# Graph attention: the turns of a group's head on VectorE, and the head's five pieces behind batches 4 to 8

## The reference

```python
h = (x @ W_i).reshape(n, H, C)
es = jnp.einsum('nhc,hc->nh', h, a_src_i)
ed = jnp.einsum('nhc,hc->nh', h, a_dst_i)
e = es[src] + ed[dst]
e = jnp.where(e > 0, e, NEG_SLOPE * e)
m = jax.ops.segment_max(e, dst, num_segments=n)
p = jnp.exp(e - m[dst])
denom = jax.ops.segment_sum(p, dst, num_segments=n)
alpha = p / denom[dst]
msg = alpha[:, :, None] * h[src]
out = jax.ops.segment_sum(msg, dst, num_segments=n)
```

## Time and profile before

| what | before |
|---|---|
| median of 3 runs | 10096.06 us (10090.6 to 10096.87) |
| the profiled execution | 10127.15 us |
| its span in the profile | 10125.4 us |
| granted TensorE clock, mean | 0.63 |
| PE, DVE, ACT, POOL busy | 55%, 52%, 46%, 49% |
| DMA | 985 MB, mean 97 GB/s |

### The profile page before, as it was taken

One profiled execution on the slowest core, in us unless ns is written; L12 is line 12 of the kernel. 1 busy time (PEld: TensorE's weight loads), 2 busy tenths in 40 slices (PEclk: granted clock), 3 DMA queues, 4 the chain that ended last, 5 costly groups with the idle time before them and its releaser, 6 DMA issues.

```text
span 10125.4 us, 129123 instructions
## 1 busy us (share of the span) xinstructions
PE 5609.1 (55%) x33883; PEld 4488.5 (44%) x33883; DVE 5300.4 (52%) x12476; ACT 4632.1 (46%) x8410; POOL 4936.4 (49%) x5153
## 2 busy tenths in 40 slices
PE   3999899734544545444455545544434444444446
PEld 2777666524444444443444444444423333333334
DVE  5888611335555555554555555555634444444445
ACT  2555300245555555553555555555434444444444
POOL 1000100356666666662566666666466666666660
PEclk9999899755555555555555555555555555555557
DMA  2333355134433434332344434443322222222221
GB/s 83 139 140 140 128 190 190 36 101 102 107 102 102 102 102 104 105 103 61 94 103 107 103 101 103 103 107 102 81 71 70 76 71 70 75 71 70 71 75 33
DMA packets 600502, 985.17 MB, mean 97 GB/s; under 512 B 330887, under 2 KB 454493, under 8 KB 560781
## 3 DMA queue, kind: packets, MB, share of 16 engines
q1 hardware_dynamic: 216924, 540.94, 16.1%
q0 software_dynamic: 163376, 356.21, 15.4%
q10 hardware_dynamic: 219648, 81.82, 3.0%
HBM read 755.78 MB, written 222.74 MB: 97 GB/s over the span
## 4 chain that ended last, share of the span: by engine, by line
PE 32%; DVE 21%; another core or an unknown queue 17%; DVEq 15%; issue 12%; ACT 1%; POOL 1%; POOLq 1%; DMA 0%; ACTq 0%; SPq 0%
PE bank L1038 12%; DVEq L1352 12%; DVE acc L1982 10%; PE bank L1264 9%; DVE arena L1969 3%; PE bank L1192 2%; PE bank L1062 2%; PE bank L1204 2%; DVEq L1982 2%; DVE bank L1938 2%; DVE arena L1940 1%; DVEq L1974 1%; DVE x_mem L1628 1%; PE bank L1174 1%
## 5 line engine op out<-in xcount | busy, mean ns | idle before, releaser
L704 POOL DMA_INDIRECT arena<-row_table,staged_idx x4980 | 4700.9, 944 | 3090.9 <-issue 1750.2
L1264 PE MATMUL bank<-arena 128*128 128x136 f32 x9984 | 2491.5, 430 | 1535.2 <-DVE acc L1982 739.9
L1264 PEld LDWEIGHTS bank<-arena 128*128 128x128 f32 x9984 | 2206.2, 317 | 1707.3 <-issue 1684.6
L1982 DVE TENSOR_TENSOR acc<-acc,bank 128x136 f32 x4992 | 1476.5, 296 | 2126.1 <-issue 822.6
L861 ACT ACTIVATE pick_dist<-col,dst_local 128x128 bf16<-128x128 f32 x4992 | 1521.8, 388 | 562.8 <-remote 492.0
L1038 PE MATMUL bank<-arena 128*128 128x385 bf16 (+1 forms) x7448 | 1324.8, 327 | 37.4 <-DVE arena L1722 20.9
L813 ACT COPY x_mem<-bank 128x384 f32<-128x384 f32 x416 | 198.9, 478 | 1813.1 <-remote 1159.1
L1038 PEld LDWEIGHTS bank<-arena 128*128 128x128 bf16 x7448 | 701.9, 98 | 458.5 <-issue 21.3
L648 POOL TENSOR_TENSOR arena<-acc,node_stat 128x896 f32 x14 | 23.9, 1709 | 1675.0 <-POOLq L660 988.0
L1969 DVE TENSOR_TENSOR arena<-arena,bank 128x528 f32<-128x528 f32 x1248 | 832.1, 687 | 0.7
L1204 PE MATMUL bank<-ident,x_mem 96*128 96x96 f32 x1664 | 364.7, 374 | 741.9 <-DVE x_mem L1630 574.4
(11 more groups left out here) (371 smaller groups left out, 5507.7 us busy)
## 6 DMA issues: line engine op xcount, KB each, us to landing
arena<-dst_rows SPq DMA_DIRECT2D x156, 1024.0 KB
cell_rows<-arena SPq DMA_DIRECT2D x75, 1568.0 KB, 5.1
arena<-cell_rows SPq DMA_DIRECT2D x75, 1568.0 KB, 6.6
edge_stats<-x_mem ACTq DMA_DIRECT2D x416, 192.0 KB
arena<-row_table,staged_idx POOLq DMA_INDIRECT x4980
x_mem<-in_edge_attr SPq DMA_DIRECT2D x208, 192.0 KB
x_mem<-segment_flags SPq DMA_DIRECT2D x416, 96.0 KB
arena<-change_rows SPq DMA_DIRECT2D x312, 64.0 KB
```

The costliest lines, as they stand in the source:

```text
L704: pool.indirect_dma_start(gathered[:, at, :], None, table, bass.IndirectOffsetOnAxis(staged_idx[:, at:at + 1], 0)).then_inc(att_gathered[n ...
L1264: mm = pe.matmul(region(k)[:, 0:ROW], pick[:, k, :], gathered[:, b * GROUP + k, :], start=True, stop=True)
L1982: done = dve.tensor_tensor(row, row, region(m * BATCH + k), ALU.add)
```

## The change

TensorE's four turns are taken out, with their semaphores. VectorE turns by its own transposes of 32x32 blocks: the scores straight into PSUM (`score_rows`, 32 partitions, one bank), the ends of the slots and the crossings into SBUF, the maxima back into PSUM (`back`). The scans go on reading rows in PSUM. `cross` grows from 4 to 32 partitions, and `row_ends` and `cross_rows` lie in the scratch memory. In all groups, ahead or not, the five pieces stand behind batches 4 to 8 (m = 3 to 7). TensorE waits for `scored` ahead of the first destination scores of a group, since these overwrite what score_edges reads. The head of a layer's first group, ahead of its batches, has the same pieces and turns.

The diff, cut to its core (turn_ends, turn_crossings and turn_maxima of TensorE go as turn_scores does; of VectorE's pieces only the new text is shown):

```diff
         end_flag = over(1024, GROUP, 2, HEADS * P)
         seg_f = over(2048, GROUP, 512)
         seg_m = over(2560, GROUP, 512)
+        score_rows = bank[0:GROUP, 3, :]
         raw, score = (over(3584 + n * P, P, HEADS, GROUP) for n in range(2))
+        back = bank[:, 3, 0:P].rearrange("p (h s) -> p h s", h=HEADS)
+        row_ends = over(3840, GROUP, 2 * GROUP)
+        cross_rows = over(3840 + 2 * GROUP, GROUP, 2 * GROUP)
         prob = bank[:, 1, 0:HEADS * GROUP].rearrange("p (h s) -> p h s", h=HEADS)
         masks = sb("masks", [HEADS, 2, 3, GROUP + 1])
         carry_f = sb("carry_f", [HEADS, GROUP + 1])
         carry_b = sb("carry_b", [HEADS, GROUP + 1])
-        cross = sb("cross", [HEADS, 2, GROUP])
+        cross = sb("cross", [GROUP, 2, GROUP])
...
-                def turn_scores(head):
-                    pe.wait_ge(att.scored, head + 1)
-                    for h in range(HEADS):
-                        mm = pe.transpose(bank[0:GROUP, 3, h * P:(h + 1) * P], score[:, h, :], ident[:, :])
-                    mm.then_inc(att.score_rows, 1)
...
                 def score_some(first, last, slot, turned):
+                    if first == 0:
+                        pe.wait_ge(att.scored, turned // 2)
                     for j in range(first, last):
                         if j % (QG // 2) == 0:
                             pe.wait_ge(att.turned, turned + j // (QG // 2) + 1)
...
                     slot = it * (2 * GROUP) + (b + 2) * GROUP
-                    late = 0 if ahead else 3
                     for m in range(NBATCH):
                         sum_batch(G, b, m)
-                        if head and m == 2 + late:
-                            turn_scores(G + 1)
-                        if head and m == 3 + late:
-                            turn_ends(G + 1)
-                        if head and m == 4 + late:
-                            turn_crossings(G + 1)
-                        if head and m == min(5 + late, NBATCH - 1):
-                            turn_maxima(G + 1)
                         if n < STATS_LAYERS and m in (4, 5):
...
+                def turn_scores():
+                    then()
+                    for q in range(P // GROUP):
+                        dve.transpose(score_rows_h[:, :, q * GROUP:(q + 1) * GROUP],
+                                      score[q * GROUP:(q + 1) * GROUP, :, :])
+                    then()
+
+                def first_scans(b, use):
                     dve.wait_ge(att_flags[b], 48 * (n * PAIRS + 1) + use * 48)
+                    dve.tensor_tensor_scan(seg_f, start_flag[:, b, :], score_rows, FAR, ALU.add, ALU.max)
+                    dve.tensor_tensor_scan(seg_m[:, ::-1], end_flag[:, b, ::-1], score_rows[:, ::-1], FAR,
+                                           ALU.add, ALU.max)
+                    then()
+                    dve.transpose(row_ends[:, 0:GROUP],
+                                  seg_f_h.rearrange("s h e -> s e h")[:, ::-1, :][:, 0:GROUP // HEADS, :])
+                    dve.transpose(row_ends[:, GROUP:2 * GROUP],
+                                  seg_m_h.rearrange("s h e -> s e h")[:, 0:GROUP // HEADS, :])
+                    then()
+
+                def carries(b):
                     dve.tensor_tensor_scan(carry_f[:, 1:GROUP + 1], masks[:, b, 1, 0:GROUP],
+                                           row_ends[0:HEADS, 0:GROUP], carry_f[:, 0:1], ALU.add, ALU.max)
+                    dve.tensor_tensor_scan(carry_b[:, 0:GROUP][:, ::-1], masks[:, b, 2, 0:GROUP][:, ::-1],
+                                           row_ends[0:HEADS, GROUP:2 * GROUP][:, ::-1], FAR, ALU.add, ALU.max)
+                    then()
+                    dve.tensor_tensor(cross[0:HEADS, 0, :], carry_f[:, 0:GROUP], masks[:, b, 0, 0:GROUP], ALU.add)
+                    dve.tensor_tensor(cross[0:HEADS, 1, :], carry_b[:, 1:GROUP + 1], masks[:, b, 0, 1:GROUP + 1],
+                                      ALU.add)
+                    then()
+                    dve.tensor_copy(carry_f[:, 0:1], carry_f[:, GROUP:GROUP + 1])
+                    dve.transpose(cross_rows, cross[:, :, :].rearrange("p m s -> p (m s)"))
+                    then()
+
+                def last_scans(b):
+                    dve.tensor_tensor(score_rows[:, 0::P], score_rows[:, 0::P], cross_rows[:, 0:HEADS], ALU.max)
+                    then()
+                    dve.tensor_tensor(score_rows[:, P - 1::P], score_rows[:, P - 1::P], cross_rows[:, GROUP:GROUP + HEADS], ALU.max)
+                    then()
+                    dve.tensor_tensor_scan(score_rows, start_flag[:, b, :], score_rows, FAR, ALU.add, ALU.max)
+                    then()
+                    dve.tensor_tensor_scan(seg_m[:, ::-1], end_flag[:, b, ::-1], score_rows[:, ::-1], FAR,
                                            ALU.add, ALU.max)
+
+                def turn_maxima():
+                    then()
+                    for q in range(P // GROUP):
+                        dve.transpose(back[q * GROUP:(q + 1) * GROUP, :, :],
+                                      seg_m_h[:, :, q * GROUP:(q + 1) * GROUP])
+                    then()
+
+                def shift_scores(b, slot):
...
                     weigh(G, b, 1)
-                    late = 0 if ahead else 3
                     for m in range(NBATCH):
                         if m + 2 < NBATCH:
                             weigh(G, b, m + 2)
                         add_batch(G, slot, m)
-                        if head and m == 0 + late:
+                        if head and m == 3:
                             score_edges(G + 1, 1 - b, use)
-                        if head and m == 1 + late:
-                            first_scans(G + 1, 1 - b, use)
-                        if head and m == 2 + late:
-                            carries(G + 1, 1 - b)
-                        if head and m == 3 + late:
-                            last_scans(G + 1, 1 - b)
-                        if head and m == min(5 + late, NBATCH - 1):
-                            shift_scores(G + 1, 1 - b, slot + GROUP)
+                        if head and m == 4:
+                            turn_scores()
+                            first_scans(1 - b, use)
+                        if head and m == 5:
+                            carries(1 - b)
+                        if head and m == 6:
+                            last_scans(1 - b)
+                        if head and m == 7:
+                            turn_maxima()
+                            shift_scores(1 - b, slot + GROUP)
                         if n < STATS_LAYERS and m in (2, 6):
```

71 lines of the change are left out of this document (11 added, 60 removed).

## The result

The changed kernel took 10,568.52 us (median of 4 runs, 10,553.25 to 10,582.18), the kernel before 10,094.72 (4 runs). The ratio is 1.0475, with a 95% interval of 1.0462 to 1.0487: 4.7% slower.

The account below looks back on a forecast made before the run. GpSimd's gathers and TensorE's held signals were taken as the bound, not VectorE or TensorE. +347 us in layers 1 and 2, +66 in layer 3 and -24 at layer starts gave +389, so 10,485 us; range 10,200 to 10,850.

Parts of the forecast that it names:

- The boundary: Between last add and rescale: turn of maxima 1.2, shift 0.8, handshake 1.0, lengthening the path by 3.0 us per group.
- ScalarE's picks ahead of the copy: Layers 1 and 2: the statistics' copy waits behind the last picks, so first sums come 3.0 to 3.7 us later; 3.5 taken.
- The turns: VectorE's eleven new transposes cost 3.0 us, with drains 3.5 us per group; bounds 2 and 8.
- The chain without gathers: Group time without held signals: 42.1 us in layers 1 and 2, 35.8 in layer 3.
- The hold: TensorE's signals, held during a 16-gather run, leave VectorE standing 10 us in layers 1 and 2, 12 in layer 3.
- Rival B: VectorE's turn waits were the bound and the holds go with them: 4.1 us less per group, 9,470 us; chance 0.06.
- The sum in layers 1 and 2: Chain 42.1 plus 10 of standing is 52.1 us per group against 48.7: +3.4 for 102 groups, +347 us.
- Layer 3: Chain and standing give 47.8 us, today's period; part of the boundary adds 1.3 us for 51 groups, +66 us.
- rival A: GpSimd's pauses become fewer, two runs of 16 gathers per group instead of 3.3 runs: -275 us, 9,820; chance 0.19.
- the prediction's own sign of being wrong: The rescale period falling below 48 us; first place to look is the number of GpSimd's pauses per group.
- The starts of layers 2 and 3: Each layer's start no longer waits for TensorE's turns: -8 us three times, -24 us.
- GpSimd's stop ahead of the first sums' gather: Idle stretch of 4 to 7 us before the gather that the next group's first sums release; all below 4.1 before.

Follow-up runs that it names:

- turns_mid: The changed kernel with all five pieces one batch earlier, behind batches 3 to 7: 10,166.15 us, ratio 1.0040 to the kernel before.
- shift_last: The kernel before, turns still on TensorE, with only the shift of the scores moved from behind batch 6 to behind batch 8: 10,427.39 us, ratio 1.0301.
- turns_twice: The changed kernel with each of the eight 32x128 transposes done twice, with a drain between: 11,426.48 us, ratio 1.1281 to the kernel before.
- place_first: The changed kernel with ScalarE placing the first half's scan values right behind the first picks in layers 1 and 2: 10,826.03 us, ratio 1.0675 to the kernel before.
- turns_only: The changed kernel's turns on VectorE, but the five pieces back behind batches 1, 2, 3, 4 and 6: 10,120.71 us, ratio 0.9994 to the kernel before.
- copies_first: The changed kernel with ScalarE copying the turned statistics ahead of the last quarter's picks in layers 1 and 2: 10,605.95 us, ratio 1.0472 to the kernel before.
- turns_by_layer: Turns on VectorE, pieces in the old order in layers 1 and 2 and behind batches 4 to 8 in layer 3: 10,197.81 us, ratio 1.0075 to the kernel before.

## Why the prediction was right, and where it was not

The forecast was 10,485, against 10,568.5. The direction and the mechanism are right. The sum for layers 1 and 2 came out 1.65 us per group too low, its terms did not simply add under the gathers, and layer 3 went the other way. Part of the nearness is luck: layers 1 and 2 grew by 515 us where 347 were forecast, layer 3 shrank by 38.5 where it was to grow by 66, and the two misses, +168 and -105, mostly cancel.

**The boundary, +3.0 us.** Right: 0.24 to 3.18, of which 1.33 are the turn of the maxima. That it lies on the path in layers 1 and 2 is shown from both sides, by turns_mid (4.4 us of the 5.0 gone) and shift_last (+2.5 with one piece moved).

**ScalarE's picks ahead of the copy, +3.5 us.** Right without gathers: in the last group but one of layer 1 the first add stands 7.50 us behind the rescale, before 4.01. With gathers the first sums do start 3.3 us later, but before they were not what the first add waited for: it stood 6.24 us behind the rescale already, with the sums started at 1.55. So it came 0.95 us later, and taking the picks out of the way gave 0.7 to 0.8 us of period. A term of the chain was added to the hold in full, where the hold covers most of it.

**The turns, +3.5 us in the chain.** The size is right, 3.2 us of transposes (0.30 and 0.19 forecast; 0.32 and 0.21 measured). The chain without gathers, forecast as 42.1 and 35.8, came to 43.05 and 35.27. What it costs under gathers depends on the place: nothing in the old order, and in the late order more than itself (turns_twice, 1.8 times). The Trainium skill ("VectorE: DVE Perf Modes", The three transpose paths) gives 0.311 us for a 128x128 bf16 transpose on VectorE; a block of 32 partitions and 128 fp32 elements, from SBUF to PSUM, took 0.316 and 0.322 here, nearly the same for a quarter of the partitions.

**The hold, +10 us.** VectorE stands 3.63 + 6.35 = 9.98 us in the first half of the group shown, as forecast; in the median it is 7.5 us in layer 1, about 9 in layer 2 and 5.1 in layer 3 (12 forecast). And the forecast put all of it down to held signals. The first 3.6 us are the scan waiting for ScalarE. place_first took that wait away and the stand moved into the held signal (8.48 us in that group), so the sum survives and the working was half right. The Trainium skill ("SBUF - State Buffer", Who interferes with whom) has the sentence that PE never waits on anyone among the consequences of its rule on SBUF ports. The prediction drew from it that no signal is held; it does not say that, and these rows neither support nor refute it. What they show is that 15.7 us pass between the recorded end of TensorE's sums and VectorE's add, with 16 gathers running, 8.5 of them with VectorE standing, and that with half of the gathers the same add follows its weigh by 0.17 us. Rival B, which needed the holds to go, did not come.

**The sum in layers 1 and 2.** 52.1 forecast, 53.75 measured. By the forecast's own terms it is 43.05 of chain (42.1) and 10.7 on top of it (10). Put against the kernel before, 2.9 us of boundary and 0.8 of copies are 3.7 of the 5.05 us; 1.3 are left, for which the forecast had no term. turns_twice points to the work in the second half, which costs more than its own time, but no run took these 1.3 us apart.

**Layer 3.** 49.1 forecast, 46.9 measured: here rival A came true, which has 47, and the prediction's own sign of being wrong, a period below 48, was met in this layer (which had 47.8 before). GpSimd settled into two runs per group, 20 and 12 gathers, 2.0 pauses where it had 3.0 (counting those above 0.5 us). The turns alone, in the old order, already bring two runs and 47.17 us (turns_only), as rival A has it, so the late order is not what is needed for it. Nor is the late order enough. Three other kernels with the same instructions in layer 3 have 48.72 (copies_first), 48.49 (turns_by_layer) and 49.13 us (place_first), with 2.7 to 2.9 pauses, and the groups of the first two wander between 45.6 and 51.1 us. In the changed kernel they lie between 46.5 and 47.4 from the third on. Again there are two kinds of groups: where the fifth batch's signal comes inside a run of gathers, a group of these three kernels takes 47.1 to 47.4 us, and where it comes at the end of one, 49.0 to 49.4. The changed kernel has only the first kind in this layer. The code differs only ahead of the layer, so something there must decide which rhythm it falls into; what, no run shows. That is 1.6 to 2.2 us per group, 80 to 110 us in all. The forecast's 49.1 is near the other rhythm, but not for a reason that it gave.

**The signs.** The starts of layers 2 and 3 are 9.1 and 16.4 us shorter (8 forecast), that of layer 1 7.4. GpSimd's stop ahead of the first sums' gather was forecast as 4 to 7 us; it is most often 7.3 in layers 1 and 2, up to 10.8, and 3.2 in layer 3. Shift to first add was forecast as 4 us or more; it is 8.9 in the boundary shown.

## What to carry to other kernels

In a loop whose slowest engine can only be fed by the next round's first step, ask what stands behind the last item of a round: in layers 1 and 2 here, work and handshakes there were added to the round, and one item earlier they were nearly free (4.4 us of 5.0). Before a wait is removed, find what would end the stand instead; two waits that cost 7.6 us a group before, and one of 3.6 us found later, were worth nothing or less; for the last one the rows show why, the signal behind it was late anyway. And a period that is a rhythm of runs and pauses should be read in several kernels before a small gain in it is believed.

## What was not expected of the hardware

TensorE's late signals end in different places. In half of the groups of layers 1 and 2 the fifth batch's comes behind the last gather of a run, 3.2 us in the group shown. In layer 3 of the changed kernel it does so in none of 46 groups. VectorE, TensorE (the sums of the fifth batch) and GpSimd:

```profile
8964.69 0.30 DVE L1958 TENSOR_TENSOR acc<-acc,bank 128x136 f32 x1 [7.42 <-remote]
```

```profile
8952.95 1.17 PE L1240 MATMUL bank<-arena 128*128 128x136 f32 x8 [0.49 <-issue]
```

```profile
8965.56 0.94 POOL L707 DMA_INDIRECT arena<-row_table,staged_idx  x1 [0.30 <-issue]
8966.81 0.94 POOL L707 DMA_INDIRECT arena<-row_table,staged_idx  x1 [0.30 <-issue]
```

VectorE sees the signal 10.6 us behind the end of the sums, but it comes in the middle of a run, just in time for the next four gathers to follow without a pause; so a run of 20 comes about. "Held until the run is over" is too simple, and what holds the signal is not settled by these runs. That half of the gathers take 7 us off a group of layer 1 and 10 off one of layer 3, with VectorE's work unchanged, shows only that the gathers have to do with it. The second surprise is the price of more work on VectorE in the late order, 5.0 to 5.3 us for 2.9 in layers 1 and 2.
